# The eight-batch AdaLN attention block: row maxima go to the other layout through DRAM and ScalarE instead of TensorE

## The reference

```
mod = (silu(c) @ wmod).reshape(8, 6, 1, 256)          # sa, ca, ga, sb, cb, gb
ga, gb = sign * max(|.|, 0.25)
h = layernorm(x) * (1 + ca) + sa
scores = (h * w_lhs) @ (h * w_rhs)^T                   # 1024 x 1024 of each batch
x = x + ga * softmax(scores) @ h
h = layernorm(x) * (1 + cb) + sb
x = x + gb * (relu(h @ W1 + b1) @ W2 + b2)             # 256 -> 1024 -> 256
```

## Time and profile before

| what | value |
|---|---|
| median of three runs | 678.67 us |
| the profiled execution | 679.18 us |
| its span from first to last instruction | 677.4 us |
| share of the span in which TensorE is busy | 99% |
| VectorE, ScalarE, GpSimd | 81%, 74%, 44% |
| granted TensorE clock | 1.00 |
| a pass of the loop (batches 2 to 6) | 80.4 us |

### The profile page before, as it was taken

One profiled execution on the slowest core, in us unless ns is written; L12 is line 12 of the kernel. 1 busy time (PEld: TensorE's weight loads), 2 busy tenths in 40 slices (PEclk: granted clock), 3 DMA queues, 4 the chain that ended last, 5 costly groups with the idle time before them and its releaser, 6 DMA issues.

```text
span 677.4 us, 13532 instructions
## 1 busy us (share of the span) xinstructions
PE 672.5 (99%) x4551; PEld 620.4 (92%) x4551; DVE 545.9 (81%) x1139; ACT 500.2 (74%) x749; POOL 295.2 (44%) x311
## 2 busy tenths in 40 slices
PE   9999999999999999999999999999999999999998
PEld 8688889998999999999999989999899999999897
DVE  4798889887899879998799887988789987778321
ACT  2376787976889777895878949888688976747563
POOL 3551365225353345442645235542535334615544
PEclk9999999999999999999999999999999999999999
DMA  8131664237632377124671256513763246311210
GB/s 295 55 81 62 194 188 148 72 97 237 194 96 74 123 238 231 48 89 149 202 210 62 93 186 195 145 62 124 216 195 84 75 146 197 97 41 65 85 48 31
DMA packets 72897, 88.57 MB, mean 131 GB/s; under 512 B 6880, under 2 KB 64800, under 8 KB 72864
## 3 DMA queue, kind: packets, MB, share of 16 engines
q1 hardware_dynamic: 72864, 88.15, 41.6%
HBM read 51.66 MB, written 36.47 MB: 130 GB/s over the span
## 4 chain that ended last, share of the span: by engine, by line
PE 99%; DVE 0%; DMA 0%; issue 0%; SPq 0%
PE col L662 9%; PE col L661 9%; PE col L660 9%; PE acc L582 8%; PE acc L583 8%; PE acc L588 8%; PE score L766 8%; PE score L762 8%; PE score L763 8%; PE score L650 4%; PE score L651 4%; PE score L649 4%; PE score L755 4%; PE score L623 2%; PE score L551 1%; PE score L727 1%
## 5 line engine op out<-in xcount | busy, mean ns | idle before, releaser
L1249 POOL TENSOR_TENSOR hid_lo<-hid,hid_hi 128x512 fp32r<-128x512 f32 x127 | 175.9, 1387 | 258.3 <-ACT hid_hi L791 257.6
L787 ACT ACTIVATE hid<-col,b1T 128x512 f32<-128x512 f32 x128 | 87.1, 681 | 72.6 <-PE col L662 67.8
L582 PE MATMUL acc<-W2hi,hid_hi 128*128 128x256 f32 x480 | 118.0, 280 | 0.0
L583 PE MATMUL acc<-W2lo,hid_hi 128*128 128x256 f32 x480 | 116.6, 277 | 0.0
L762 PE MATMUL score<-V,Phi 128*128 128x258 f32 x448 | 108.7, 281 | 0.0
L763 PE MATMUL score<-V,Phi 128*128 128x256 f32 x448 | 108.5, 281 | 0.0
L662 PE MATMUL col<-h2hi,W1lo 128*128 128x512 f32 x256 | 101.0, 395 | 0.0
L660 PE MATMUL col<-h2hi,W1hi 128*128 128x512 f32 x256 | 100.7, 393 | 0.0
L661 PE MATMUL col<-h2lo,W1hi 128*128 128x512 f32 x256 | 100.7, 393 | 0.0
L791 ACT ACTIVATE hid_hi<-hid 128x512 fp32r<-128x512 f32 x128 | 81.0, 633 | 23.2 <-PE acc L588 15.6
L582 PEld LDWEIGHTS acc<-W2hi,hid_hi 128*128 128x128 f32 x480 | 90.3, 188 | 1.4
(11 more groups left out here) (168 smaller groups left out, 1476.5 us busy)
## 6 DMA issues: line engine op xcount, KB each, us to landing
block_rows<-blocks SPq DMA_DIRECT2D x29, 512.0 KB, 2.8
blocks<-block_rows SPq DMA_DIRECT2D x116, 128.0 KB, 2.9
x_cur<-x SPq DMA_DIRECT2D x16, 512.0 KB, 3.9
ln_t<-x SPq DMA_DIRECT2D x14, 512.0 KB, 4.8
score_blocks<-stage SPq DMA_DIRECT2D x14, 512.0 KB, 2.9
S<-score_blocks SPq DMA_DIRECT2D x56, 128.0 KB, 3.0
S<-quarter_blocks SPq DMA_DIRECT2D x56, 96.0 KB, 2.6
out<-x_mlp SPq DMA_DIRECT2D x8, 512.0 KB, 5.3
```

The costliest lines, as they stand in the source:

```text
L582: nc.tensor.matmul(o, hi, W2hi[:, it, :], start=(it == 0 and (apart or t % 2 == 0)), stop=False, skip_group_check=True)
L583: nc.tensor.matmul(o, hi, W2lo[:, it, :], start=False, stop=False, skip_group_check=True)
L787: nc.scalar.activation(hid[:, n % 2, :], col[n % 2][:], ACT.Relu, bias=b1T[:, n % FT:n % FT + 1]).then_inc(col_read, 1)
L1249: G.tensor_tensor(hid_lo[:, n % RING, :], hid[:, n % 2, :], hid_hi[:, n % RING, :].bitcast(F32), ALU.subtract).then_inc(hid_lo_done, 1)
```

## The change

Batch 0 keeps the transposes. In the seven others `MB` is gone from TensorE's list. In its place come:

- `MW.n` on SyncE: waits for `row_max` and stores its four columns to `max_rows` in DRAM, one number (4 bytes) at a time, 512 of them, so that they lie there by tile and row.
- `MR.n` on SyncE: waits for that store and loads the 512 numbers into each of the 128 partitions, into a part of `stage` (n = 0) or `S` (n = 1) that is free at that time.
- `MP.n` on ScalarE: waits for that load and copies 128x512 to `max_ps`.

`SB` reads the same place as before and finds the tiles in the order of `MAX_ORDER`. All five tables have new orders as well.

```diff
+    max_rows = nc.dram_tensor("max_rows", [2, HT, P], F32, kind="Internal").ap()
...
+        max_in = [stage[:, 0].rearrange("p u v t r -> p (u v t r)")[:, 0:HR], s_flat[:, at:at + HR]]
...
+                    elif kind == "MW":
+                        sp.wait_ge(max_ready, 2 * b + n - 1)
+                        sp.dma_start(max_rows[n].rearrange("a p -> p a"), row_max[:, n * HT:(n + 1) * HT], allow_slow_non_contiguous=True).then_inc(max_stored, 16)
+                    elif kind == "MR":
+                        sp.wait_ge(max_stored, 16 * (2 * b + n - 1))
+                        sp.dma_start(max_in[n], max_rows[n].rearrange("a p -> (a p)").partition_broadcast(P)).then_inc(max_loaded, 16)
...
-                            o, most = max_ps[:, j * P:(j + 1) * P], n * HT + MAX_ORDER[j % HT]
-                            if ph is PH["first"]:
-                                o, most = first_max[n][:, j % HT * P:(j % HT + 1) * P], j
-                            last = nc.tensor.transpose(o, row_max[:, most:most + 1].broadcast_to([P, P]), ident[:])
+                            o = first_max[n][:, j % HT * P:(j % HT + 1) * P]
+                            last = nc.tensor.transpose(o, row_max[:, j:j + 1].broadcast_to([P, P]), ident[:])
...
+                    elif kind == "MP":
+                        act.wait_ge(scores_read, T * b + HT * (n + 1))
+                        act.wait_ge(max_loaded, 16 * (2 * b + n - 1))
+                        nc.scalar.activation(max_ps[:, n * HR:(n + 1) * HR], max_in[n], ACT.Copy).then_inc(max_done, 1)
...
-                        most = max_ps[:, n * P:(n + 1) * P].unsqueeze(1)
+                        place = h * HT + MAX_ORDER[t]
+                        most = max_ps[:, place * P:(place + 1) * P].unsqueeze(1)
```

More of the change, by code:

```diff
@@ L53 @@
     "act": """
[L54 removed]
+        WS.0 N1.0+ EU.0 EU.1 EX.0 EU.2 EX.1 EU.3 EX.2 L1.0+ EX.3 TH.0+ N1.1+ EX.4 EX.5 RL.0+ EX.6 N2.0 EX.7
         TH.1+ RL.1+ MC.0 T2.0
@@ L57 @@
     "dve": """
-        MF.0 SC.0 L1.0+ SC.1 WQ.0 SC.2 GA.0 BH.0+ SC.3 SC.4 SU.0 SU.1 SC.5 SU.2 SC.6 SU.3 SC.7 SB.0 SB.1 SB.2
-        L1.1+ SB.3 AV.0 AV.1 SB.4 SB.5 BH.1+ AV.2 AV.3 TH.0+ SB.6 AV.4 SB.7 AV.5 XG.0 AV.6 TH.1+ XG.1 AV.7
-        VO.0 T2.0
+        MF.0 SC.0 L1.0+ GA.0 SC.1 SC.2 WQ.0 SC.3 BH.0+ SC.4 SC.5 SU.0 SU.1 SC.6 SU.2 SC.7 SU.3 SB.0 SB.1 SB.2
+        L1.1+ SB.3 AV.0 SB.4 AV.1 SB.5 AV.2 BH.1+ TH.0+ AV.3 SB.6 AV.4 SB.7 XG.0 XG.1 AV.5 AV.6 TH.1+ AV.7
+        T2.0 VO.0
     """,
     "pool": """
-        L1.0+ WS.0 WQ.0 XC.0 L1.1+ XC.1 XC.2 XC.3 L2.0 L2.1
+        L1.0+ WQ.0 WS.0 XC.0 XC.1 XC.2 L1.1+ L2.0 XC.3 L2.1
     """,
     "sp": """
-        SH.0+ GB.0 AM.0 XT.1+ RH.0+ SH.1+ RH.1+ X0.0+
+        GB.0 AM.0 SH.0+ XT.1+ RH.0+ SH.1+ RH.1+ X0.0+
     """,
@@ L100 @@
     "pe": """
-        SC.0 SC.1 F.0- SC.2 SC.3 F.1- SC.4 F.2- F.3- G.0- F.4- G.1- SC.5 SC.6 F.5- SC.7 G.2- G.3- F.6- F.7-
-        MB.0 G.4- G.5- G.6- G.7- F.8- F.9- AV.0 F.10- F.11- F.12- G.8- G.9- AV.1 AV.2 MB.1 G.10- AV.3 G.11-
-        F.13- G.12- AV.4 F.14- F.15- AV.5 G.13- AV.6 G.14- AV.7 G.15-
+        SC.0 SC.1 F.0- SC.2 SC.3 F.1- SC.4 F.2- F.3- G.0- SC.5 F.4- G.1- SC.6 SC.7 F.5- G.2- G.3- G.4- F.6-
+        F.7- G.5- F.8- G.6- G.7- F.9- F.10- AV.0 F.11- G.8- F.12- AV.1 AV.2 G.9- AV.3 F.13- G.10- G.11- AV.4
+        F.14- G.12- F.15- G.13- AV.5 AV.6 AV.7 G.14- G.15-
     """,
     "act": """
-        N2.1- F.0- V.0 F.1- F.2- F.3- VN.1 F.4- T2.1- N1.0+ F.5- V.1 F.6- L1.0+ F.7- EX.0 EX.1 SM.0 F.8- F.9-
-        SM.1 EX.2 F.10- SM.2 EX.3 SM.3 F.11- TH.0+ N1.1+ EX.4 SM.4 F.12- EX.5 F.13- SM.5 EX.6 MC.0 N2.0 SM.6
-        TH.1+ F.14- EX.7 SM.7 F.15- RL.0+ RL.1+ T2.0
+        N2.1- V.0 F.0- F.1- F.2- F.3- VN.1 F.4- T2.1- N1.0+ L1.0+ MC.0 V.1 F.5- F.6- F.7- MP.0 F.8- EX.0 EX.1
+        SM.0 SM.1 F.9- F.10- EX.2 SM.2 EX.3 F.11- SM.3 TH.0+ MP.1 N1.1+ F.12- EX.4 SM.4 F.13- EX.5 SM.5 N2.0
+        EX.6 TH.1+ SM.6 EX.7 RL.0+ SM.7 F.14- F.15- RL.1+ T2.0
     """,
     "dve": """
[L111 to L114, removed]
+        B2.1- SC.0 XG.2- SC.1 XG.3- SC.2 ST.0 SC.3 QT.0 SC.4 ST.1 V.0 ST.2 L1.0+ ST.3 SC.5 VL.1 SC.6 SC.7 QT.1
+        MX.0 T2.1- BH.0+ V.1 VP.0+ MX.1 SB.0 SB.1 OUT.0- SM.0 SB.2 SB.3 MX.2 SM.1 AV.0 L1.1+ SM.2 SM.3 AV.1
+        AV.2 SB.4 BH.1+ AV.3 SB.5 SM.4 XG.0 SB.6 TH.0+ AV.4 SB.7 SM.5 B2.0 TH.1+ XG.1 SM.6 AV.5 SM.7 AV.6 AV.7
+        OUT.1- T2.0
     """,
     "pool": """
-        F.0- XC.0 F.1- F.2- F.3- L1.0+ F.4- F.5- XC.1 F.6- F.7- F.8- F.9- XC.2 F.10- XC.3 L1.1+ F.11- F.12-
+        XC.0 XC.1 F.0- F.1- F.2- L1.0+ F.3- F.4- F.5- F.6- F.7- XC.2 F.8- F.9- L1.1+ F.10- F.11- XC.3 F.12-
         L2.0 F.13- F.14- F.15- L2.1
@@ L147 @@
     "sp": """
-        S2.1- AM.0 R2.1- X1.0 SW.0 QW.0 GA.0- QR.0 SR.0 SW.1 SR.1 QW.1 QR.1 O0.0- GB.0 S2.0 R2.0 O1.0- O1.1-
+        GA.0- S2.1- AM.0 X1.0 R2.1- QW.0 SW.0 QR.0 SR.0 SW.1 MW.0 SR.1 MR.0 QW.1 QR.1 O0.0- GB.0 MW.1 MR.1
+        S2.0 R2.0 O1.0- O1.1-
     """,
@@ L167 @@
     "sp": """
-        S2.1- R2.1- GA.0- O0.0- O1.0- OT.2- OT.3-
+        S2.1- GA.0- R2.1- O0.0- O1.0- OT.2- OT.3-
     """,
@@ L713, in part @@
                     elif kind == "MB":
-                        if ph is PH["first"]:
[L716 to L722, removed]
+                        pe.wait_ge(scores_read, T * b + HT * (n + 1))
                         for j in range(n * HT, (n + 1) * HT):
-                            o, most = max_ps[:, j * P:(j + 1) * P], n * HT + MAX_ORDER[j % HT]
-                            if ph is PH["first"]:
-                                o, most = first_max[n][:, j % HT * P:(j % HT + 1) * P], j
-                            last = nc.tensor.transpose(o, row_max[:, most:most + 1].broadcast_to([P, P]), ident[:])
+                            o = first_max[n][:, j % HT * P:(j % HT + 1) * P]
+                            last = nc.tensor.transpose(o, row_max[:, j:j + 1].broadcast_to([P, P]), ident[:])
                         last.then_inc(max_done, 1)
```

55 lines of the change are left out of this document (28 added, 27 removed).

## The result

| | before | after |
|---|---|---|
| median of the runs | 678.82 us (4 runs) | 766.15 us (4 runs) |
| ratio, with 95% interval | | 1.1289 (1.1275 to 1.1302) |
| span of the profiled execution | 677.4 us | 766.3 us |
| mean granted TensorE clock | 1.000 | 0.955 |

What follows compares the result with a forecast made beforehand. It took gap-free TensorE (busy 672.5 of 677.4 us) as the bound, with the transfers hidden: 679.18 - 6.2 = 673.0 us profiled, 672.5 as median of the runs. The range was 671.8 to 677.3 us.

Steps and rivals of the forecast that it cites:

- What is removed: TensorE, seven batches: 14 groups of four transposes (MB) at 0.44 us each, 6.2 us, all on the path.
- The store: Maxima to DRAM, 512 packets of 4 bytes: bounds 1.9 and 3.9 us, taken as 3.1.
- The load: Maxima from DRAM into all partitions, 128 packets of 2 KB: bounds 3.7 and 5.5 us, taken as 4.2.
- `SR.1` behind the store: SyncE's queue: SR.1 lands at 30.2 of the pass, no more than 0.7 us late for MX.1.
- The spare time: Loop pass: store and load may take 8.3 to 8.4 us before TensorE waits at AV.0.
- the first chain: Loop pass, MX.0 through transfers, SB.0, exp and Phi to AV.0 at 38.8: 1.0 us to spare.
- rival 2: VectorE becomes the bound, as steps moved ahead of SB.0 take cover from AV.0: 676 us, chance 0.10.
- Batch 1, "so it has more": Batch 1: AV.0 stands 2.8 us later than in the loop, so the transfers have more spare time.
- Rival 1: Late transfers make TensorE wait before AV.0: 683.3 us with a 5.9 us store; chance 0.17.
- the second chain: Loop pass: MX.2 ends 44.3, maxima land 51.7, SB.4 at 53.1, AV.4 needs Phi at 59.8; 1.7 us to spare.
- The new orders at nothing: All engines: the sum charges nothing for the new tables' orders, only small differences in batch 0 within the range.
- The chances: Whole kernel: faster 0.83, the same 0.05, slower 0.12.

Runs made afterwards that it cites:

- r2_16B: Changed kernel with the maxima stored as 128 packets of 16 bytes, put in order by ScalarE's copy: 676.36 us, ratio 0.9957 to the kernel before.
- r7_apart: Changed kernel with the same 512 packets of 4 bytes stored 64 bytes from each other: 675.82 us in one run, beside 679.44 of the kernel before.
- m1_dma: No computation, single DMAs each waited for: 512 packets of 4 bytes took 9.0 us side by side, 2.1 at 512 bytes from each other.
- r3_srfirst: Changed kernel with SyncE issuing SR.1 ahead of MW.0 in the loop and batch 7: 753.02 us in one run.
- r5_mix: The 16-byte store kernel with batch 0's old orders and, in batch 1, G.8 behind AV.0 on TensorE: 675.90 us, ratio 0.9958 to the kernel before.
- r6_mix2: 16-byte store and batch 0's old orders, with G.8 and G.9 between F.11 and AV.0 in batch 1: 675.99 us, ratio 0.9948 to the kernel before.
- r4_busy: Changed kernel with useless matmuls in TensorE's three waits of a loop pass: 756.9 us in one run, clock 0.989 against 0.955.
- r1_orders: Kernel before with the new orders of all engines, transposes kept, no store, load or copy of maxima: 682.99 us, ratio 1.0061.
- m3_dma: No computation, single stores of 4-byte packets each waited for: side by side from 16 / 32 / 64 / 128 partitions 2.2 / 5.4 / 7.9 / 8.8 us.

## Why the prediction was wrong, step by step

- **What is removed: right.** 0.44 us for each `MB`. Versions with the same orders and a quick store are 6.6 us (r2_16B) and 7.2 (r7_apart, one run) below the one with transposes; I had 6.2.
- **The store: the step that failed.** "The store, 512 packets of 4 bytes ... 3.9 in all. I take 3.1" measured 7.8 to 11.1 us. I priced it by the mean packet of the queue, and its upper end was no bound: its row was of packets mostly of a kilobyte. The packets themselves are cheap, 2.1 to 2.6 us for 512 of them apart. What I had not in the sum is that small writes beside each other in DRAM hinder each other. No row of the trace before showed one, and the honest upper end was open.
- **The Trainium skill on it: the right advice, neither the reason nor the price.** That page of the Trainium skill ("DMA: Bandwidth & Descriptors", "Rules for kernel authors") has one descriptor for each element, and the trace agrees: 82,272 packets against 72,864 are 9,408 more, 14 times 672, the 512 and 128 of the two transfers and 16 for each of them at its end. But it is not their number that costs: 512 such packets took 9.0 us side by side and 2.1 when 512 bytes apart (m1_dma), and the page's line on what is under 512 B does not tell the one from the other.
- **The load: right.** 3.3 to 5.8 us, median 4.8; 12 of 14 lie within 3.7 to 5.5.
- **`SR.1` behind the store, "no more than 0.7 late": wrong by ten times.** It was 7.3 us late, by the same mis-sized store. With `SR.1` ahead of the store the time is 13 us less (r3_srfirst, one run).
- **The spare time, 8.3 to 8.4 us: about right, and too wide.** With 9.1 and 5.4 us the first chain gives 14.5 - 8.3 = 6.2 us of lateness; measured 7.0. In the loop of the 16-byte versions the load is issued 2.4 us after the store and lands in 4.0 to 5.6. Where that made 7.9 in all, `AV.0` waited 0.5 to 0.7, and where it made 7.3 it did not wait (r2_16B, r5_mix, r6_mix2): the spare time is 7.2 to 7.4. `VP.0` took 2.02 instead of 1.23 (r5_mix), and VectorE waited twice for 0.3 to 0.4: some of rival 2.
- **Batch 1, "so it has more": right for `AV.0`, and not enough.** With 2.8 us more to spare and 14.3 us of transfers it was 3.1 over, and TensorE waited 1.5 us ahead of `F.10` and 1.3 ahead of `AV.0`. But it waited 4.6 us further on, for the relu that stands behind `MP.1` on ScalarE, and the batch lost 11.4 us in all.
- **Rival 1: the right mechanism, and too small in three ways.** It had chain, place and sign. Its store was 5.9, not 9.1. It counted one wait in a pass, though the same figures put the second chain, with 1.7 to spare, over its limit as well: 5.4 us more. And it had no clock, which r4_busy prices at about 2 us a pass. In batch 3 the two losses, clock included, are 7.0 + 5.4 = 12.4 of the pass's 12.9.
- **The new orders at nothing: wrong by 4 us** (r1_orders), in batches 0 to 2, which I had not gone through step by step as I had the loop.
- **The chances.** 0.12 on slower was too little for a term without any row of its kind, on the path of six passes, where 1 us more turned the sign.

## What to carry to other kernels

A transfer of single numbers has its price in where the numbers land: four numbers of a partition kept together, and put in order by the copy that is needed anyway, made a store of 9 us one of 1.4. Where a trace has no row of the kind of a new operation, the mean of other rows is not its upper end; measure it alone first, which took four stores of each kind here. And when a chain with little to spare gets a new link, look for every place in a pass where the same link stands, and for what is queued behind it.

## What the runs showed of the hardware that I had not expected

- 128 writes of 4 bytes side by side into DRAM took 8.0 to 8.8 us, 512 of them in four such rows 9.0 to 9.6, 512 of them 64 bytes apart 2.6. At 32 bytes from each other, or of 32 bytes each, 128 took 1.4 (m1_dma to m3_dma).
- Later DMAs of the same queue can be late behind such a store: four loads of `SR.1`, which land in 3.0 us, let VectorE go on only 11.8 us after the last was issued (batch 3 of the changed kernel), and with `SR.1` issued ahead of the store that wait was gone (r3_srfirst).
- A halved clock cost less than half of what it seemed to, as part of it fell into a stretch that waited for something else. It stood at 0.50 for 3 to 17 us of a pass of the loop; useless matmuls that kept it at 1.00 gave back 9 us of 766, 2 us a pass.
